# Value products of two narrow attentions split by query columns, second half one step later; the first layer's masks loaded before its attention

## The reference, cut to what matters

```python
# layer 0: causal                               # layer 1: not causal
scores = einsum('bthd,bshd->bhts', q, k)/sqrt(8)  scores = einsum('bhqd,bhkd->bhqk', q, k) * 8**-0.5
scores = where(causal_mask, -inf, scores)         scores -= max(scores, -1)
attn = softmax(scores)                            attn = exp(scores) / maximum(sum, 1e-12)
out = einsum('bhts,bshd->bthd', attn, v)          ctx = einsum('bhqk,bhkd->bhqd', attn, v)
```

## Time and profile before

| what | us |
| --- | --- |
| median of three runs | 3595.76 |
| profiled execution, whole | 3575.11 |
| its span | 3573.2 |
| first layer's attention, first slot to last division | 69.7 to 555 |
| second layer's attention | about 884 to 1597 |
| PE busy in the span | 2981.4 |
| DVE busy | 2616.7 |
| ACT busy | 2150.4 |

### The profile page before, as it was taken

One profiled execution on the slowest core, in us unless ns is written; L12 is line 12 of the kernel. 1 busy time (PEld: TensorE's weight loads), 2 busy tenths in 40 slices (PEclk: granted clock), 3 DMA queues, 4 the chain that ended last, 5 costly groups with the idle time before them and its releaser, 6 DMA issues. The chain is left out here.

```text
span 3573.2 us, 51682 instructions
## 1 busy us (share of the span) xinstructions
PE 2981.4 (83%) x18320; PEld 1203.9 (34%) x18320; DVE 2616.7 (73%) x6042; ACT 2150.4 (60%) x2740; POOL 451.6 (13%) x633
## 2 busy tenths in 40 slices
PE   5999997896999999985799998967469988889836
PEld 2333333443122222223355555545322222222214
DVE  6999973666999999946566666640868888888821
ACT  2566673323377777773355555522369999899822
POOL 2000001333000000000000000014220011102023
PEclk7899998997799999997899999978779999999968
DMA  4443202343211111000000000011362222221102
GB/s 146 58 106 62 33 13 48 64 80 112 30 27 27 22 22 22 12 3 3 31 1 1 1 7 7 1 54 50 106 140 33 33 33 39 27 30 23 53 24 74
DMA packets 172975, 148.27 MB, mean 41 GB/s; under 512 B 79672, under 2 KB 130632, under 8 KB 172720
## 3 DMA queue, kind: packets, MB, share of 16 engines
q1 hardware_dynamic: 168624, 137.21, 19.2%
q0 software_dynamic: 4096, 7.78, 0.7%
HBM read 95.13 MB, written 49.68 MB: 41 GB/s over the span
## 5 line engine op out<-in xcount | busy, mean ns | idle before, releaser
L1321 ACT ACTIVATE a_probs<-a_scores 128x1024 f32<-128x1024 f32 (+3 forms) x896 | 791.5, 932 | 374.1 <-PE a_scores L1203 233.9
L1344 DVE TENSOR_REDUCE a_part_max<-a_slot_ps 128x1 f32<-128x512 f32 x1280 | 798.6, 684 | 30.9 <-PE a_slot_ps L1181 29.6
L2341 DVE TENSOR_TENSOR a_probs<-a_logit_ps,a_gate 128x1024 f32<-128x1024 f32 x512 | 602.4, 1219 | 98.8 <-ACT a_gate L2200 97.5
L1181 PE MATMUL a_slot_ps<-a_k_op,a_q_op 48*128 48x512 bf16 (+3 forms) x1792 | 579.1, 380 | 95.6 <-DMA a_mask_wide<-in_mask_wide 17.9
L2205 ACT ACTIVATE a_probs<-a_probs 128x2048 f32<-128x2048 f32 x256 | 488.1, 1907 | 7.7 <-DVE a_probs L2341 7.6
L1203 PE MATMUL a_scores<-a_q_op,a_k_op 51*128 51x512 bf16 (+3 forms) x1792 | 452.4, 361 | 7.1 <-ACT a_probs L1321 6.1
L1223 PE MATMUL a_o_ps<-a_probs,a_v_op 128*32 128x512 f32 (+3 forms) x3584 | 437.9, 561 | 1.2 <-ACT a_o_sb L1308 0.6
L1181 PEld LDWEIGHTS a_slot_ps<-a_k_op,a_q_op 48*128 48x128 bf16 x1792 | 150.2, 94 | 697.5 <-DVE a_part_max L1344 469.2
L2106 PE MATMUL a_logit_ps<-space 96*128 96x512 bf16 x1024 | 303.3, 387 | 71.2 <-DVE a_probs L2341 62.4
L2200 ACT ACTIVATE a_gate<-a_diff_ps 128x1024 f32<-128x1024 f32 x256 | 261.6, 1022 | 55.2 <-PE a_diff_ps L2106 47.5
L2119 PE MATMUL a_o_ps<-a_probs,a_v_op 128*32 128x512 f32 x2048 | 274.0, 607 | 7.0 <-DVE a_o_sb L2334 3.1
(11 more groups left out here) (400 smaller groups left out, 3758.3 us busy)
## 6 DMA issues: line engine op xcount, KB each, us to landing
e_coef<-coef_dram SPq DMA_DIRECT2D x16, 1024.0 KB, 9.9
a_q_op<-scratch_q SPq DMA_DIRECT2D x384, 32.0 KB
a_k_op<-scratch_k SPq DMA_DIRECT2D x384, 32.0 KB
scratch_q<-p_parts SPq DMA_DIRECT2D x24, 384.0 KB, 3.4
scratch_k<-p_parts SPq DMA_DIRECT2D x24, 384.0 KB, 3.4
space<-scratch_k SPq DMA_DIRECT2D x192, 32.0 KB
space<-scratch_g SPq DMA_DIRECT2D x192, 32.0 KB
space<-scratch_q SPq DMA_DIRECT2D x192, 32.0 KB
```

What stands on the lines that cost most here:

```text
L1181: nc.tensor.matmul(out[:, 0:width], q_op[g][r0:r0 + MAX_ROW, e, qt * P:(qt + 1) * P], k_op[g][r0:r0 + MAX_ROW, e, kh * CH:kh * CH + width] ...
L1321: nc.scalar.activation(probs[gs % NB][:, 2 * e:2 * e + 2, off:CH], scores[e][:, :, off:CH], ACT.Exp, scale=scale).then_inc(probs_done, 1)
L1344: nc.vector.tensor_reduce(part_max[u % 2][:, kh, col:col + 1], slot[:, 0:w], axis=AX.X, op=ALU.max).then_inc(slot_done, 1)
L2341: nc.vector.tensor_tensor(probs[gs % 4][:, m, :, :], logit_ps[m][:], gate[gs % 2][:], op) \
```

## The change

Each call of `values` is now one of two parts: part 0 takes the first half of the step's columns, part 1 the rest, eight instructions each. Part 0 of a step is issued one step later as before, but between the scores of e = 1 and slot d; part 1 is issued two steps later, behind slot b of e = 0. Only part 1 counts in `pv_done`. The masks' three loads move from the start of layer 0's attention into `load_early` at chunk 3 of its projection.

```diff
     def load_early(self, sp, c):
+        if self.causal and c == 3:
+            for n, tile in (("ident2", self.ident2), ("mask_b2", self.mask_b2), ("mask_wide", self.mask_wide)):
+                sp.dma_start(tile[:], self.consts[n]).then_inc(self.masks_loaded, 16)
         self.load_qk(sp, 0, range(2 * (c - 3), min(2 * (c - 2), len(PAIR_PARTS))))
...
-            if shape.causal:
-                for n, tile in (("ident2", ident2), ("mask_b2", mask_b2), ("mask_wide", mask_wide)):
-                    sp.dma_start(tile[:], consts[n]).then_inc(masks_loaded, 16)
...
-            def values(u, n):
+            def values(gs, part):
+                u, n = divmod(gs, S)
                 hq, kb = shape.steps[n]
                 g, off = u % GROUPS, shape.off(hq, kb)
-                te.wait_ge(probs_done, (u * S + n + 1) * 2)
-                if n == 0:
-                    te.wait_ge(v_spread, u + 1)
-                if kb == 0 and u * 2 + hq > 0:
-                    te.wait_ge(o_copied, u * 2 + hq)
+                middle = (off + CH) // 2
+                first, last = ((off, middle), (middle, CH))[part]
+                if part == 0:
+                    te.wait_ge(probs_done, (gs + 1) * 2)
+                    if n == 0:
+                        te.wait_ge(v_spread, u + 1)
+                    if kb == 0 and u * 2 + hq > 0:
+                        te.wait_ge(o_copied, u * 2 + hq)
                 for j in range(H):
-                    mm = nc.tensor.matmul(o_ps[32 * j:32 * (j + 1), off:CH], v_op[g][:, kb, 32 * j:32 * (j + 1)],
-                                          probs[(u * S + n) % NB][:, j, off:CH], start=kb == 0, stop=n in shape.half_end)
-                mm.then_inc(pv_done, 1)
+                    mm = nc.tensor.matmul(o_ps[32 * j:32 * (j + 1), first:last], v_op[g][:, kb, 32 * j:32 * (j + 1)],
+                                          probs[gs % NB][:, j, first:last], start=kb == 0 and part == 0,
+                                          stop=n in shape.half_end and part == 1)
+                if part == 1:
+                    mm.then_inc(pv_done, 1)
...
                         mm.then_inc(scores_ready, 1)
+                        if e == 1 and gs > 0:
+                            values(gs - 1, 0)
                         for v, s in todo[cut[2 * e + 1]:cut[2 * e + 2]]:
                             a_slot(v, s)
-                    if n > 0:
-                        values(u, n - 1)
-                    elif u > 0:
-                        values(u - 1, S - 1)
+                        if e == 0 and gs > 1:
+                            values(gs - 2, 1)
...
-            values(UNITS - 1, S - 1)
+            values(UNITS * S - 2, 1)
+            for part in range(2):
+                values(UNITS * S - 1, part)
             o_turn(UNITS - 1, 1)
```

More of the change, by code:

```diff
@@ L1046, with __init__ @@
 class NarrowOperands:
-    def __init__(self, nc, ctx, name, shape, qs, ks, vs):
+    def __init__(self, nc, ctx, name, shape, qs, ks, vs, consts):
         def sb(n, shp, dt=FP32):
@@ L1060, in __init__ @@
         self.qs, self.ks, self.vs = qs, ks, vs
+        self.causal, self.consts = shape.causal, consts
+        self.ident2, self.mask_b2 = (sb(n, [P, 2, P], BF16) for n in ("ident2", "mask_b2"))
+        self.mask_wide = sb("mask_wide", [P, CH])
+        self.masks_loaded = nc.alloc_semaphore(f"{name}_masks_loaded")
     def load_qk(self, sp, u, parts=range(len(PAIR_PARTS))):
@@ L1096, in narrow_attention @@
         ident = consts["ident"]
-        ident2, mask_b2 = (sb(n, [P, 2, P], BF16) for n in ("ident2", "mask_b2"))
-        mask_wide = sb("mask_wide", [P, CH])
+        ident2, mask_b2, mask_wide, masks_loaded = operands.ident2, operands.mask_b2, operands.mask_wide, operands.masks_loaded
         R, NB = GROUPS, 4
@@ L1111, in narrow_attention @@
         o_ps = ps("o_ps", [P, CH])
-        ones_loaded, masks_loaded, preset = sem("ones_loaded"), sem("masks_loaded"), sem("preset")
+        ones_loaded, preset = sem("ones_loaded"), sem("preset")
         max_loaded = [sem(f"max_loaded{i}") for i in range(R)]
@@ L3102, in four_layers @@
                 shape = NarrowShape(True)
-                operands = NarrowOperands(nc, inner, "a0", shape, scratch[0], scratch[1], scratch_v)
+                operands = NarrowOperands(nc, inner, "a0", shape, scratch[0], scratch[1], scratch_v, consts)
                 project(nc, "p0", x, mv, rstd, a["L0_Wq"], a["L0_Wk"], a["L0_Wv"], scratch[0], scratch[1], scratch_v, ident,
@@ L3115, in four_layers @@
                 shape = NarrowShape(False)
-                operands = NarrowOperands(nc, inner, "a1", shape, scratch[0], scratch[1], scratch_v)
+                operands = NarrowOperands(nc, inner, "a1", shape, scratch[0], scratch[1], scratch_v, consts)
                 project(nc, "p1", xn1, mv, rstd, a["L1_Wq"], a["L1_Wk"], a["L1_Wv"], scratch[0], scratch[1], scratch_v, ident,
```

## The result

The changed kernel takes 3621.35 us (median of four runs, 3613.33 to 3629.01), the kernel before in the same comparison 3594.69 us (3592.12 to 3598.79). The ratio is 1.0072, 95% interval 1.0049 to 1.0094: slower by 0.7%, clear of the noise, and above the predicted range. The two comparisons say 20 to 27 us more.

The account below looks back on a forecast made before the run. DVE was taken to bound layer 1, with PE and DVE about equal in layer 0 after the change. Masks -3.3, layer 0 -4.4, tails -3 and layer 1 +5 made -5.7 us: 3590 us, range 3568 to 3614.

Parts of the forecast that it names:

- DVE needs 2.49. So DVE still ends last: Layer 1's step: four reductions take DVE 2.49 us, PE after the change 2.42, so 0.07 us to spare.
- DVE's is 26.1: Layer 0's unit of 28.49 us: DVE's work is 26.1 us, the other 2.4 us idle.
- the two waits at the turns of the halves: Layer 1: DVE idles 0.3 us at each half, 0.6 a unit against 0.27 before; +5 us over 14.7 units.
- PE's 26.4 as floor: Layer 0: with the added work and two copy waits, PE needs 26.4 to 26.6 us a unit; gain at most 30 us.
- the wait at the division: Layer 0: the long wait before the division at n = 6 about halves, while small ones before c and d appear.
- The price of d behind half 0: Layer 0: d runs after part 0 beside the next a, costing 0.14 us of PE time a step.
- The masks: Start of layer 0's attention: first slot 3.5 us earlier, less 0.2 us of projection delay; sum -3.3 us.
- rival C: The early masks bring nothing because something else starts late; 3593 us, chance 0.08.
- B: Slower: PE becomes the bound of layer 1's step, and layer 0 loses 17 us; 3615 us, chance 0.22.
- A: Even spacing feeds DVE in layer 0, gaining 1.2 us a unit, -17.4 us; layer 1 unchanged; 3572 us, chance 0.28.
- the price of a second emptying: Each step: the array runs empty 0.11 us before values once more, part of the split's 0.25 us.
- d's lost partner: Slot d no longer runs beside a score: one pass more, 0.21 us a step in layer 1, 0.14 in layer 0.

Follow-up runs that it names:

- e8: The changed kernel unedited, timed again beside the kernel before on a second chip: ratio 1.0057.
- e4: The changed kernel with slot d issued ahead of values part 0 instead of behind it: 3559.28 us, ratio 0.9905 to the kernel before.
- e7: The changed kernel with slot d ahead of part 0 and each half's last step as one whole values call: 3552.98 us, ratio 0.9885 to the kernel before.
- e9: The kernel before, but values calls from each half's second key block on compute only the first half of their query columns: ratio 0.9883.
- e1: The kernel before with only the masks' loads moved into the projection, values whole: 3594.0 us, ratio 1.0001.
- e2: The kernel before with values split as in the change in layer 0 only, masks loaded as before: ratio 1.0016.
- e3: The kernel before with values split as in the change in layer 1 only, masks loaded as before: median 3611.36 us, ratio 1.0048.
- e5: The changed kernel with both values parts issued together at the step's end, behind slot d, where the whole call stood: ratio 1.0006 to the kernel before.
- e12: The changed kernel with slot d ahead of values part 0 in the first two units of layer 1: ratio 1.0024 to the kernel before.

## Why the prediction was wrong

**Forecast: 5.7 us less; measured 20 to 27 more.** By place in the two profiled executions, the forecast was -9.5 us up to the expert layer and +3.7 measured; +5 for layer 1's units and +7.7 measured; nothing for layer 1's start and +6.8 measured (+14 in e8). Layer 1's tail, forecast at -1.2, stayed as it was. The 20 us that are left between these executions lie between and behind the two attentions, where no code differs.

1. **The step that failed: "DVE needs 2.49. So DVE still ends last", and "DVE's is 26.1" in layer 0.** From four reductions back to back and 552.88 busy us of 560 the forecast took DVE as the bound of layer 1 and PE's 0.58 us before slot d as slack. e4, e7 and e9 show 2.39 to 2.41 us with the same reductions, so before was in a loop of PE and DVE. That hid the large thing in this change, 1.6 us a unit that a split can give (41.93 to 40.32), and why the change does not get it: its step is 2.47 us (PE's forecast 2.42 and 0.05 more), so DVE, which could take 2.41, can't catch up after a wait. Its 42.48 are 40.32 + 16 x (2.47 - 2.41) + 1.03 of listed waits + 0.17 unexplained. In the sum itself this error costs little: the step came within 0.02 us of the forecast, by luck, and the two waits at the turns of the halves are 0.62 us together where 0.6 was forecast. The third wait, 0.41, was not in the sum.
2. **Layer 0, the largest part: -0.3 us a unit forecast, +0.28 measured.** The forecast had the right pieces: PE's 26.4 as floor, the wait at the division gone (3.9 left of 20.7), small ones before masked slots. But it added up listed waits alone, and by these the unit is indeed no worse (31.5 us where 33.1 had been). It is the 26.1 us that did not stay: without its listed waits a unit is 28.49 - 2.36 = 26.13 us in before and 28.77 - 2.26 = 26.51 in the change, and 25.9 in e7 (27.25 - 1.32) and e9 (26.73 - 0.81), with the same work for DVE. So before had gaps in it already that no list shows, and the change adds 0.38 us. The price of d behind half 0 was put at 0.14 us of PE's time a step, 1.7 us a unit; e4 gives back 1.45. The forecast had it in PE's floor and took it for covered by slack. In the tail +2 us were measured where -1.8 was expected; its cause is open.
3. **A missing term: layer 1's start at 1.2 GHz.** No step asked what PE's added work costs where the granted clock is 0.50. It is +6.8 us in the profiled execution and +14 in e8 (55.75 against 41.77 in e1). Its length differs from run to run, and it likely spreads the runs of the change: the fastest of e8 (3605.83) has a mean granted clock of 0.922, the slowest (3627.0) 0.915.

**The masks.** First slot forecast at 66.2 to 66.6, measured 67.69. The wait for the masks has gone, as forecast: the slot follows the start of the attention's queues by 0.1 us instead of 3.5. But these queues came up at 67.5 instead of 66.1. The three issues held SP's queue 2.1 us instead of the forecast's 1.3 (0.86, 0.66, 0.47 with the gaps); how much of the 1.4 us is theirs is open, since in e2 and e3, with the masks as before, the queues came up at 67.1. In e1, 1.3 us of the gain are left at the second `row_max`, under what the runs can tell: rival C in effect.

**The rivals.** B had the right outcome and nearly the number (3615), by a mechanism that holds in part. PE's side did set the step, 2.47 us against DVE's true 2.41, but it did not pass 2.49 at full clock, and the surcharge for narrow tiles that B feared does not exist (e5). A, the even spacing that feeds DVE, is what e4 and e7 show, and in layer 0 by its very number (1.17 and 1.24 us a unit, forecast 1.2); layer 1's 1.4 and 1.6 us a unit come on top. In the change slot d's place takes both away.

**Right.** 0.57 us for a half, the price of a second emptying, d's lost partner, the wait for the copy at each half (0.27 us, forecast 0.2 to 0.3) and DVE's wait behind it, the division's wait in layer 0.

## What to carry to other kernels

Add up one turn of the loop by which buffers come back (issue, work ahead in the queue, consumer, release) before an engine that looks busy is called the bound; and compare start-to-start times of its operations, not busy shares, since records of neighbours overlap. Here a long block cut into parts paid when each part stood behind the slots that the other engine waits for (e4); ahead of one of them it cost more than the cut gave. Price added work at the clock of each stretch, the half-clock start too.

## What was not expected of the hardware

- A reduction over 128x512 from PSUM lasts 0.69 us in the records and starts every 0.603 us when its slot is there. 0.623 us already meant waiting.
- Column-tiled float32 products of 256 columns cost 0.57 us a call between other work and 1.00 us for two calls in a row (e5): 0.14 us goes with the change to and from them.
- TensorE stayed at 1.2 GHz for 111 us behind the first `row_max` with 20.00 busy us of 20 (e3), in its slowest execution, and for 20 to 22 us with the same products in another order (e4, e5, e12). What of the order does it is open.
- In e9, with fewer columns, the clock fell back in the midst of layer 1, and there are such falls in layer 0 too. Its windows from 1390 us on:

```profile
1390.00:1395.00 5.00, 4.44 (x34) 1.44 (x33) 4.90 (x13) 3.30 (x5) 0.00 (x0) 1.00 0.00 2
1395.00:1400.00 5.00, 5.00 (x29) 1.15 (x28) 4.54 (x8) 3.69 (x4) 1.95 (x5) 0.51 0.03 6
```
